# A graph attention layer: exponentials straight from kept h, a third bank for h, and a new order of every engine's opening

## The chip, the cores and the metric

One core of a Trainium2 chip runs the whole layer. The metric is the device time of the execution in microseconds, taken several times; a profiled execution gives the trace.

## What is computed

The input x has 4096 rows (nodes) of 256 features, adj is a 4096 x 4096 0/1 matrix with about 1 in 256 set.

```
hn  = max(layernorm(x), 0)
h   = hn @ W.T                     # 4096 x 256
src = h @ a1;  dst = h @ a2
e   = leaky_relu(src[:, None] + dst[None, :], 0.2)
e   = where(adj == 0, -9e15, e)
out = x + softmax(e, axis=1) @ h
```

The kernel uses exp(leaky_relu(s + d)) = max(exp(s + d), exp(0.2 (s + d))). With a common factor taken out, the weight of an edge is p_scale(d) * max(c(s), g(d)), where c = exp(-0.8 s - bias), g = exp(0.8 d + bias) and p_scale = exp(0.2 d + bias') up to the constants; bias comes from an upper bound of all d, so that nothing overflows. The row's sum of weights is an extra column of the product.

## The kernel before

The 4096 nodes are 32 tiles of 128 (T = 32). The first stage (the opening) makes h; the second (the products) makes attention @ h in NG = 4 groups of RB = 8 row blocks, each group running over all 32 tiles.

**The opening, for each tile t.** VectorE takes mean and variance (`stats_of`, `gather`). For a batch of tiles (`BATCHES`: 0-1, 2-3, 4-7, 8-11, 12-17, 18-23, 24-31) ScalarE takes the root (`std_of`), VectorE its reciprocal (`rstd_of`) and, for batches that ScalarE normalises from, `shift_of`. `normalise` writes hn_sb; the lists `BY_VECTOR`, `BY_SCALAR` and `BY_GPSIMD` say on which engine. TensorE transposes the tile into a PSUM bank (`turn`). ScalarE writes the fp16 high part with Relu (`split_hn_hi`), VectorE the low part (`split_hn_lo`). TensorE projects with three products, high part by the weights' high part (`project_hi`), high by low (`project_w_lo`), low by high (`project_lo`), two matmuls each, into a bank for h: 6 or 7 in turn, so that `project_hi(t)` waits until `keep_h(t - 2)` has emptied it. ScalarE's `keep_h` writes h_sb, whose columns F and F + 1 are s and d. `value_hi` and `value_lo` make the fp16 parts of h in pairs of tiles, the operands of the products; `HIGH_BY_SCALAR` and `HIGH_BY_GPSIMD` say who does the first.

**The weights W.** TensorE transposes W at the start. ScalarE scales it into w_hi in two halves and two extra columns (L531, L534, L537), VectorE makes w_lo of each. The instruction for w_lo's extra columns waits for `w_hi_ready` to reach KC = 2, that is for both halves.

**The turn to the products.** When h of tile 27 is kept, VectorE takes the largest d so far (d_up, L935), TensorE spreads it and the d of the last four tiles (`turn_d`, `spread_d`), and VectorE makes d_top, d_early, d_safe and exp_bias. `exp_c` turns s of the first 8 row blocks, which came back by way of DRAM into c_row, into c, in four parts. Two VectorE instructions make the arguments for g and p_scale of tiles 0 to 3 in gp_args, and one Exp on ScalarE (`exp_gp`) makes both; the same again for tiles 4 to 31 later. A small Exp on table_ready (L620) stands ahead of keep_h(28).

**The products.** For each tile VectorE makes p_sb = min(max(c, g), adjacency bits) (`weights_part`, `edge_weights`), ScalarE p_hi = p_sb * p_scale (`hi_part`, `split_hi`), VectorE p_lo (`low_part`, `split_lo`), and TensorE adds 8 x 3 products of 257 or 256 columns (`sums`). Tiles 0 and 1 are done in parts, to start sooner. adj is loaded by SyncE into a ring of four slots, each as soon as the weights of the tile four earlier are made. For the later groups c is computed once for all tiles (c_col), transposed by VectorE (c_blocks), stored by GpSimd to c_flat and loaded by SyncE into c_row between the adjacency loads.

Every engine runs its own program, written out instruction by instruction up to the end of group 0, and waits on semaphores. ScalarE, VectorE, GpSimd and TensorE take their instructions strictly in the written order. The later groups run in loops that the change does not touch.

## Time and profile before

| | |
|---|---|
| median of 3 runs | 384.48 us (384.39 to 384.5) |
| profiled execution | 384.67 us, span 382.9 us |
| TensorE busy | 376.8 us (98%) |
| VectorE busy | 363.9 us (95%) |
| ScalarE busy | 195.1 us (51%) |
| GpSimd busy | 42.0 us (11%) |
| first product starts | 40.84 us |

The span is the stretch from the first to the last instruction of the trace, and the execution's time holds some 1.8 us more. In rows of a timeline the first number is the start in us from the span's start, the second the time from there to the end of the group, then engine, line, operation, output<-inputs, the shape and how many instructions are merged; brackets give the idle time before and what ended it. PE is TensorE, PEld its weight loads, ACT ScalarE, DVE VectorE, POOL GpSimd, SP SyncE.

### The profile page before, as it was taken

The numbers are of one execution on the slowest core, as the hardware profiler recorded it, in microseconds if no ns is written. First come the engines' busy times: TensorE is split into PE (matmuls) and PEld (weight loads), VectorE is DVE, ScalarE is ACT, GpSimd is POOL, SyncE is SP. The second block draws the span as 40 slices with busy tenths as digits, with TensorE's granted clock in tenths as the row PEclk, the third lists the DMA queues.
The fourth block names the chain that finished last, engine by engine and source line by source line (L and its number), as shares of the span: only waits on it lengthen the run. The fifth ranks groups of instructions, "written<-read, shape, count | busy, mean of one in ns | idle before, by whom it ended". The sixth has DMA issues, their size and how long they took to land.

```text
span 382.9 us, 9216 instructions
## 1 busy us (share of the span) xinstructions
PE 376.8 (98%) x3358; PEld 330.7 (86%) x3358; DVE 363.9 (95%) x458; ACT 195.1 (51%) x271; POOL 42.0 (11%) x66
## 2 busy tenths in 40 slices
PE   8999899999999999999999999999999999999996
PEld 6788688888888888888888888888888888888885
DVE  4999999999999999999999999999987999999965
ACT  5899754744443644344445544444446443444330
POOL 3897020000000001110000002100000012100000
PEclk9999999999999999999999999999999999999999
DMA  7922476847676666776676667766665577766503
GB/s 241 370 78 56 130 235 218 287 154 238 217 236 208 205 220 214 243 229 218 220 223 207 209 217 233 236 222 225 215 205 184 168 222 240 232 220 221 165 2 110
DMA packets 27024, 78.22 MB, mean 204 GB/s; under 512 B 3956, under 2 KB 9336, under 8 KB 27000
## 3 DMA queue, kind: packets, MB, share of 16 engines
q1 hardware_dynamic: 25712, 74.72, 60.9%
q0 software_dynamic: 1280, 3.16, 2.2%
q8 instruction: 16, 0.26, 0.3%
q14 instruction: 8, 0.07, 0.1%
q10 hardware_dynamic: 8, 0.00, 0.0%
HBM read 73.66 MB, written 4.21 MB: 203 GB/s over the span
## 4 chain that ended last, share of the span: by engine, by line
PE 96%; ACT 1%; DVE 1%; DMA 1%; issue 1%; ACTq 0%
PE ps L1390 87%; PE ps L1214 2%; PE ps L1229 2%; PE ps L1235 2%; PE ps L1240 2%; DMA a_rows<-a 1%; PE ps L1179 1%; PE ps L1195 1%; DVE rows_sb L1119 0%; ACT c_row L494 0%; ACT h_sb L468 0%; ACT L620 0%; ACT p_hi L504 0%; ACTq L479 0%; DVE inv_den L1115 0%
## 5 line engine op out<-in xcount | busy, mean ns | idle before, releaser
L1390 PE MATMUL ps<-v_sb,p_hi 128*128 (+2 forms) x2048 | 251.8, 273 | 1.0 <-ACT p_hi L504 0.9
L514 ACT ACTIVATE p_hi<-p_sb,gp 128x1024 f16<-128x1024 f32 x126 | 144.4, 1149 | 166.6 <-DVE p_sb L785 140.0
L1390 PEld LDWEIGHTS ps<-v_sb,p_hi 128*128 128x128 f16 x2048 | 199.6, 98 | 26.9 <-issue 1.2
L792 DVE SCALAR_TENSOR_TENSOR p_lo<-p_sb,gp,p_hi 128x1024 f16<-128x1024 f32 x126 | 160.8, 1277 | 7.1 <-ACT p_hi L514 6.7
L785 DVE SCALAR_TENSOR_TENSOR p_sb<-c_row,gp,adj_sb 128x1024 f32<-128x1024 uint32 (+1 forms) x126 | 160.5, 1278 | 0.0
L1390 PE MATMUL ps<-v_sb,p_lo 128*128 (+1 forms) x1024 | 142.7, 273 | 0.0
L1390 PEld LDWEIGHTS ps<-v_sb,p_lo 128*128 128x128 f16 x1024 | 100.0, 98 | 12.7 <-DVE p_lo L792 0.2
L452 POOL DMA_DIRECT2D out<-rows_sb x24 | 13.0, 541 | 263.1 <-DVE rows_sb L1086 262.9
L401 POOL TENSOR_SCALAR hn_sb<-x_sb,moments,rstd 128x256 f32<-128x256 f32 x17 | 21.3, 1261 | 4.3 <-DVE rstd L734 3.4
L744 DVE SCALAR_TENSOR_TENSOR hnt_lo<-ps,hnt_hi 128x256 f16<-128x256 f32 x32 | 12.9, 410 | 0.5 <-ACT hnt_hi L484 0.5
L1229 PE MATMUL ps<-w_hi,hnt_hi 128*128 128x258 f16 x64 | 12.5, 277 | 0.5 <-ACT h_sb L468 0.4
L468 ACT ACTIVATE h_sb<-ps 128x258 f32<-128x258 f32 x32 | 12.3, 388 | 1.1 <-PE ps L1240 1.1
L1235 PE MATMUL ps<-w_lo,hnt_hi 128*128 128x258 f16 x64 | 12.5, 277 | 0.0
L484 ACT ACTIVATE hnt_hi<-ps 128x256 f16<-128x256 f32 x32 | 12.1, 391 | 0.7 <-PE ps L1214 0.5
L725 DVE BATCH_NORM_STATS2 stats<-x_sb 128x6 f32<-128x256 f32 x32 | 12.3, 409 | 0.2 <-DMA x_sb<-x 0.2
L1240 PE MATMUL ps<-w_hi,hnt_lo 128*128 128x258 f16 x64 | 12.3, 274 | 0.0
L1214 PE MATMUL ps<-ident_a,hn_sb 128*128 128x128 f32 x64 | 12.0, 285 | 0.0
L1086 DVE SCALAR_TENSOR_TENSOR rows_sb<-rows_sb,inv_den,x_sb 128x256 f32<-128x256 f32 x24 | 11.4, 477 | 0.0
L757 DVE TENSOR_TENSOR v_sb<-h_sb,v_sb 128x512 f16<-128x512 f32 x16 | 10.8, 680 | 0.0
L686 ACT ACTIVATE rows_sb<-ps 128x257 f32<-128x257 f32 x24 | 7.9, 388 | 2.5 <-PE ps L1390 2.5
L1214 PEld LDWEIGHTS ps<-ident_a,hn_sb 128*128 128x128 f32 x64 | 7.8, 145 | 1.3 <-ACT hn_sb L475 0.6
L475 ACT ACTIVATE hn_sb<-x_sb,shift,rstd 128x256 f32<-128x256 f32 x14 | 8.5, 607 | 0.1
(85 smaller groups left out, 87.3 us busy)
## 6 DMA issues: line engine op xcount, KB each, us to landing
adj_sb<-adj_t SPq DMA_DIRECT2D x128, 512.0 KB, 4.8
x_sb<-x SPq DMA_DIRECT2D x7, 512.0 KB, 8.3
out<-rows_sb POOLq DMA_DIRECT2D x24, 128.0 KB, 4.3
c_row<-c_flat SPq DMA_DIRECT2D x3, 512.0 KB, 6.1
out<-rows_sb SPq DMA_DIRECT2D x8, 128.0 KB, 1.7
x_sb<-x SPq DMA_DIRECT2D x2, 256.0 KB, 3.8
c_row<-s_flat SPq DMA_DIRECT2D x1, 512.0 KB, 3.8
w_nat<-w SPq DMA_DIRECT2D x1, 256.0 KB, 2.8
```

The source lines that it names most:

```text
L401: nc.gpsimd.tensor_scalar(hn_sb[:, t % RN, :], x_sb[:, t, :], moments[:, t, 0:1], rstd[:, t:t + 1], ALU.subtract, ALU.mult).then_inc(hn_gp ...
L452: pool.dma_start(out_v[:, bass.ds(g * RB + k, 1), :], rows_sb[:, k:k + 1, 0:F])\
L468: nc.scalar.activation(h_sb[:, t, :], ps[:, bank_h + t % 2, 0:FW], ACT.Copy, scale=H_DOWN)\
L514: nc.scalar.activation(p_hi[:, u % R, :], p_sb[:, u % R, :], ACT.Copy, scale=p_scale[:, bass.ds(t, 1)])\
L744: nc.vector.scalar_tensor_tensor(out=turned("lo", t), in0=in_chunks(banks_t[t % TB]), scalar=0.0, in1=turned("hi", t), op0=ALU.max, op1=AL ...
L785: nc.vector.scalar_tensor_tensor(out=p_sb[:, u % R, :], in0=c_row[:, bass.ds(g * WG, WG)], scalar=g_col[:, bass.ds(t, 1)], in1=adj_sb[:, u ...
L792: nc.vector.scalar_tensor_tensor(out=p_lo[:, u % R, :], in0=p_sb[:, u % R, :], scalar=p_scale[:, bass.ds(t, 1)], in1=p_hi[:, u % R, :], op ...
L1214: last = nc.tensor.transpose(ps[:, banks_t[t % TB], c * P:(c + 1) * P], hn_sb[:, t % RN, c * P:(c + 1) * P], ident[:])
L1229: nc.tensor.matmul(bank_of(t), turned("hi", t)[:, c, :], w_hi[:, c, 0:FW], start=(c == 0), stop=False)
L1235: nc.tensor.matmul(bank_of(t), turned("hi", t)[:, c, :], w_lo[:, c, 0:FW], start=False, stop=False)
L1240: last = nc.tensor.matmul(bank_of(t), turned("lo", t)[:, c, :], w_hi[:, c, 0:FW], start=False, stop=(c == KC - 1))
L1390: return nc.tensor.matmul(ps[:, k, 0:width], part[:, u % R, k * P:(k + 1) * P], v_sb[:, bass.ds(t, 1), v, 0:width], start=start, stop=stop ...
```

## The change

- The two exponentials are taken by ScalarE from h_sb's column d, with scale and bias given as operands (`exp_g`, `exp_p`). gp_args and its four VectorE instructions go; one small VectorE instruction makes p_bias.
- h gets a third PSUM bank (6, 7, 4), and bank_d and bank_e become 5 and 2.
- The lists of who normalises and who makes value_hi are new, and so is the order of all instructions of ScalarE, VectorE, GpSimd and TensorE from the start to the end of group 0. GpSimd's exp_scale, den_scale and den_low now follow all its normalises and value_hi. table_ready moves into the middle of group 0.

The diff, cut to its core:

```diff
-    BY_VECTOR = [26]
-    BY_SCALAR = [0, 1] + list(range(4, 14, 2)) + [15, 19, 21, 23, 24, 25, 29]
-    BY_GPSIMD = [2] + list(range(3, 15, 2)) + [14, 16, 17, 18, 20, 22, 27, 28, 30, 31]
+    BY_VECTOR = []
+    BY_SCALAR = [1, 4, 6, 9, 10, 13, 14, 16, 19, 20, 22, 24, 26, 29, 30]
+    BY_GPSIMD = [0, 2, 3, 5, 7, 8, 11, 12, 15, 17, 18, 21, 23, 25, 27, 28, 31]
     HIGH_BY_VECTOR = []
-    HIGH_BY_SCALAR = [2, 6] + list(range(14, T, 2))
-    HIGH_BY_GPSIMD = [0, 4, 8, 10, 12]
+    HIGH_BY_SCALAR = [18, 20, 22, 24, 26, 28, 30]
+    HIGH_BY_GPSIMD = [0, 2, 4, 6, 8, 10, 12, 14, 16]
...
-        bank_w, bank_n, bank_d, bank_e = 4, 1, 4, 5
-        bank_h = 6
+        bank_w, bank_n, bank_d, bank_e = 4, 1, 5, 2
+        banks_h = (6, 7, 4)
+        HB = len(banks_h)
         banks_t = (2, 3, 1, 0)
         TB = len(banks_t)
...
+            normalise(0)
             pool.wait_ge(norms_ready, 1)
             nc.gpsimd.tensor_scalar(wa_norm[:], norms[:, 0:1], norms[:, 1:2], W_UP ** 2, ALU.mult, ALU.mult)\
                 .then_inc(pool_step, 1)
+            normalise(2)
+            normalise(3)
+            normalise(5)
+            normalise(7)
+            pool.wait_ge(wa_hi_ready, 1)
+            nc.gpsimd.tensor_copy(w2_hi[:], w_hi[:, :, F + 1:FW].to_broadcast([P, KC, P])).then_inc(w2_ready, 1)
+            value_hi(0)
+            normalise(8)
+            value_hi(2)
+            normalise(11)
+            value_hi(4)
+            normalise(12)
+            normalise(15)
+            normalise(17)
+            value_hi(6)
+            normalise(18)
+            normalise(21)
+            value_hi(8)
+            value_hi(10)
+            normalise(23)
+            normalise(25)
+            normalise(27)
+            normalise(28)
+            normalise(31)
+            value_hi(12)
+            value_hi(14)
+            value_hi(16)
             pool.wait_ge(pool_step, 1)
-            for n, factor in enumerate((-0.8, 0.8, -0.8 * H_DOWN)):
+            for n, factor in enumerate((-0.8, 0.8, -0.8 * H_DOWN, 0.2)):
                 nc.gpsimd.tensor_scalar(exp_scale[:, n:n + 1], wa_norm[:], factor / H_UP, None, ALU.mult)\
                     .then_inc(scales_ready, 1)
             pool.wait_ge(w_scale_ready, 1)
...
-            def exp_gp(tiles, n):
-                act.wait_ge(gp_args_ready, n)
-                nc.scalar.activation(gp[:, :, tiles], gp_args[:, :, tiles], ACT.Exp).then_inc(gp_ready, 1)
+            def exp_g(t0, t1):
+                act.wait_ge(c_bias_ready, 1)
+                act.wait_ge(h_kept, t1)
+                nc.scalar.activation(g_col[:, t0:t1], h_sb[:, t0:t1, F + 1], ACT.Exp,
+                                     bias=exp_bias[:, 0:1], scale=exp_scale[:, 1:2]).then_inc(g_ready, 1)
+
+            def exp_p(t0, t1):
+                act.wait_ge(p_bias_ready, 1)
+                act.wait_ge(h_kept, t1)
+                nc.scalar.activation(p_scale[:, t0:t1], h_sb[:, t0:t1, F + 1], ACT.Exp,
+                                     bias=p_bias[:, 0:1], scale=exp_scale[:, 3:4]).then_inc(p_scale_ready, 1)
...
             std_of(0)
-            act.wait_ge(w_turned, 1)
-            act.wait_ge(w_scale_ready, 1)
-            nc.scalar.activation(in_halves(w_hi)[:, 0], w_in_psum[:, 0], ACT.Copy, scale=w_scale[:, 0:1]).then_inc(w_hi_ready, 1)
-            act.wait_ge(w_turned, 2)
-            act.wait_ge(w_scale_ready, 1)
-            nc.scalar.activation(in_halves(w_hi)[:, 1], w_in_psum[:, 1], ACT.Copy, scale=w_scale[:, 0:1]).then_inc(w_hi_ready, 1)
+            split_w_hi(0)
             act.wait_ge(w_turned, KC)
             act.wait_ge(wa_scale_ready, 1)
             nc.scalar.activation(w_hi[:, :, F:FW], wa_in_psum, ACT.Copy, scale=wa_scale[:, 0:1]).then_inc(wa_hi_ready, 1)
-            normalise(0)
             std_of(1)
+            split_hn_hi(0)
             normalise(1)
-            split_hn_hi(0)
+            split_w_hi(1)
             split_hn_hi(1)
-            keep_h(0)
             std_of(2)
             split_hn_hi(2)
-            keep_h(1)
+            normalise(4)
             split_hn_hi(3)
-            normalise(4)
-            keep_h(2)
+            keep_h(0)
             normalise(6)
             split_hn_hi(4)
+            keep_h(1)
+            split_hn_hi(5)
             std_of(3)
+            keep_h(2)
...
             split_hn_hi(30)
             split_hn_hi(31)
+            keep_h(25)
+            keep_h(26)
             keep_h(27)
-            nc.scalar.activation(table_ready[:], eps_sb[:], ACT.Exp)
             keep_h(28)
             exp_c(0)
+            exp_g(0, R)
+            exp_c(1)
+            exp_p(0, R)
             keep_h(29)
-            exp_gp(slice(0, R), 1)
-            exp_c(1)
             exp_c(2)
+            exp_c(3)
             hi_part(0, 0)
-            exp_c(3)
             hi_part(0, 1)
             keep_h(30)
             hi_part(0, 2)
+            hi_part(0, 3)
             keep_h(31)
-            hi_part(0, 3)
             hi_part(1, 0)
             hi_part(1, 1)
             split_hi(2, 2, 0)
+            value_hi(18)
+            exp_g(R, T)
+            split_hi(3, 3, 0)
+            exp_p(R, T)
+            act.wait_ge(p_scale_ready, 2)
...
             act.wait_ge(c_bias_ready, 1)
             all_kept(act)
             nc.scalar.activation(c_col[:], h_sb[:, :, F], ACT.Exp, bias=exp_bias[:, 0:1], scale=exp_scale[:, 0:1])\
                 .then_inc(c_col_ready, 1)
-            exp_gp(slice(R, T), 2)
...
+            value_hi(30)
+            nc.scalar.activation(table_ready[:], eps_sb[:], ACT.Exp)
             split_hi(2, 26, 24)
...
+            def split_w_lo(c):
+                dve.wait_ge(wa_hi_ready, 1)
+                dve.wait_ge(w_hi_ready, c + 1)
+                nc.vector.scalar_tensor_tensor(out=in_halves(w_lo)[:, c], in0=w_in_psum[:, c], scalar=w_scale[:, 0:1],
+                                               in1=in_halves(w_hi)[:, c], op0=ALU.mult, op1=ALU.subtract)\
+                    .then_inc(w_lo_ready, 1)
+
...
-            dve.wait_ge(wa_hi_ready, 1)
-            for c in range(KC):
-                dve.wait_ge(w_hi_ready, c + 1)
-                nc.vector.scalar_tensor_tensor(out=in_halves(w_lo)[:, c], in0=w_in_psum[:, c], scalar=w_scale[:, 0:1],
-                                               in1=in_halves(w_hi)[:, c], op0=ALU.mult, op1=ALU.subtract)\
-                    .then_inc(w_lo_ready, 1)
-            rstd_of(1)
-            stats_of(4)
-            stats_of(5)
             dve.wait_ge(wa_scale_ready, 1)
             dve.wait_ge(w_hi_ready, KC)
             dve.wait_ge(wa_hi_ready, 1)
             nc.vector.scalar_tensor_tensor(out=w_lo[:, :, F:FW], in0=wa_in_psum, scalar=wa_scale[:, 0:1],
                                            in1=w_hi[:, :, F:FW], op0=ALU.mult, op1=ALU.subtract).then_inc(w_lo_ready, 1)
-            split_hn_lo(0)
+            split_w_lo(0)
+            rstd_of(1)
+            stats_of(4)
+            stats_of(5)
             stats_of(6)
+            stats_of(7)
             gather(4)
-            stats_of(7)
             gather(5)
             gather(6)
             gather(7)
-            split_hn_lo(1)
+            split_w_lo(1)
             stats_of(8)
             rstd_of(2)
+            split_hn_lo(0)
+            shift_of(2)
+            gather(8)
+            split_hn_lo(1)
+            stats_of(9)
             split_hn_lo(2)
-            gather(8)
-            shift_of(2)
-            stats_of(9)
             split_hn_lo(3)
             stats_of(10)
             stats_of(11)
...
+            value_lo(10)
+            value_lo(12)
             dve.wait_ge(h_kept, SOON - 1)
             nc.vector.tensor_reduce(d_most[:], h_sb[:, 0:SOON - 1, F + 1], AX.X, ALU.max).then_inc(d_most_ready, 1)
-            split_hn_lo(30)
-            split_hn_lo(31)
+            split_hn_lo(29)
             dve.wait_ge(h_kept, SOON)
...
-            dve.wait_ge(scales_ready, 5)
+            dve.wait_ge(scales_ready, 6)
             dve.wait_ge(d_safe_ready, 1)
             nc.vector.tensor_scalar(exp_bias[:], d_safe[:], exp_scale[:, 2:3], None, ALU.mult).then_inc(c_bias_ready, 1)
             dve.wait_ge(c_bias_ready, 1)
-            nc.vector.tensor_scalar(gp_args[:, 0, 0:R], h_sb[:, 0:R, F + 1], exp_scale[:, 1:2],
-                                    exp_bias[:, 0:1], ALU.mult, ALU.add).then_inc(g_args_ready, 1)
-            dve.wait_ge(g_args_ready, 1)
-            nc.vector.tensor_scalar(gp_args[:, 1, 0:R], gp_args[:, 0, 0:R], 0.25, math.log(P_UP), ALU.mult, ALU.add)\
-                .then_inc(gp_args_ready, 1)
-            value_lo(10)
+            nc.vector.tensor_scalar(p_bias[:], exp_bias[:], 0.25, math.log(P_UP), ALU.mult, ALU.add).then_inc(p_bias_ready, 1)
+            split_hn_lo(30)
+            split_hn_lo(31)
             weights_part(0, 0)
+            weights_part(1, 0)
             weights_part(0, 1)
-            weights_part(1, 0)
             weights_part(0, 2)
             weights_part(0, 3)
+            weights_part(1, 1)
             low_part(0, 0)
-            weights_part(1, 1)
             low_part(0, 1)
+            edge_weights(2, 2, 16, 0)
             low_part(1, 0)
...
+            dve.wait_ge(c_col_ready, 1)
+            nc.vector.transpose(c_blocks[:], c_col[:]).then_inc(c_blocks_ready, 1)
+            split_lo(2, 10, 8)
...
             def project_hi(t):
                 pe.wait_ge(hnt_hi_ready, t + 1)
-                if t >= 2:
-                    pe.wait_ge(*kept(t - 2))
+                if t >= HB:
...
+                pe.wait_ge(hnt_lo_ready, LAST_IN_BANK_E + 1)
                 nc.tensor.transpose(ps[:, bank_e, 0:P], d_up[:, 0:1].to_broadcast([P, P]), ident[:]).then_inc(d_turned, 1)
 
-            keep_busy(bank_h, 3)
+            keep_busy(banks_h[0], 3)
             turn(0)
             turn(1)
+            turn(2)
             project_hi(0)
+            project_hi(1)
             project_w_lo(0)
+            project_w_lo(1)
+            project_hi(2)
+            turn(3)
             project_lo(0)
-            project_hi(1)
-            project_w_lo(1)
-            turn(2)
+            project_w_lo(2)
             project_lo(1)
-            turn(3)
-            project_hi(2)
-            project_w_lo(2)
+            turn(4)
+            turn(5)
             project_lo(2)
             project_hi(3)
             project_w_lo(3)
+            turn(6)
             project_lo(3)
-            turn(4)
-            turn(5)
-            turn(6)
+            turn(7)
             project_hi(4)
             project_w_lo(4)
             project_lo(4)
-            turn(7)
             project_hi(5)
             project_w_lo(5)
...
             project_w_lo(27)
             project_lo(27)
             spread_d()
             project_hi(28)
+            turn_d()
             project_w_lo(28)
-            turn_d()
+            project_hi(29)
             project_lo(28)
-            project_hi(29)
+            project_hi(30)
+            project_hi(31)
             project_w_lo(29)
             project_lo(29)
-            project_hi(30)
             project_w_lo(30)
+            project_w_lo(31)
             project_lo(30)
-            project_hi(31)
-            project_w_lo(31)
             project_lo(31)
```

## Rows read from the trace of the kernel before

**Rows 1.** Page: busy us, share, instructions of each engine; clock in 40 slices.

```profile
PE 376.8 (98%) x3358; PEld 330.7 (86%) x3358; DVE 363.9 (95%) x458; ACT 195.1 (51%) x271; POOL 42.0 (11%) x66
...
PEclk9999999999999999999999999999999999999999
```

**Rows 2.** Timeline of TensorE, first product and two later tiles.

```profile
40.84 0.60 PE L1390 MATMUL ps<-v_sb,p_hi 128*128 128x257 f16 x4 [0.66 <-ACT p_hi L504]
...
52.55 1.92 PE L1390 MATMUL ps<-v_sb,p_hi 128*128 128x257 f16 x16
...
55.19 1.92 PE L1390 MATMUL ps<-v_sb,p_hi 128*128 128x257 f16 x16
```

**Rows 3.** Timeline of TensorE, start and end of the projections.

```profile
8.27 0.29 PEld L1214 LDWEIGHTS ps<-ident_a,hn_sb 128*128 128x128 f32 x2 [0.22 <-ACT hn_sb L475]
...
9.44 0.62 PE L1229 MATMUL ps<-w_hi,hnt_hi 128*128 128x258 f16 x2
...
9.85 0.63 PE L1235 MATMUL ps<-w_lo,hnt_hi 128*128 128x258 f16 x2
...
36.10 0.59 PE L1249 MATMUL ps<-hnt_hi,w_hi 128*128 128x512 f16 x2
```

**Rows 4.** Timeline of ScalarE at the start.

```profile
7.10 0.47 ACT L534 ACTIVATE w_hi<-ps,w_scale 128x256 f16<-128x256 f32 x1 [0.39 <-PE ps L1195]
...
8.29 0.59 ACT L475 ACTIVATE hn_sb<-x_sb,shift,rstd 128x256 f32<-128x256 f32 x1
...
9.00 0.38 ACT L484 ACTIVATE hnt_hi<-ps 128x256 f16<-128x256 f32 x1
```

**Rows 5.** Timeline of VectorE, start and end of the opening.

```profile
7.05 0.30 DVE L729 BATCH_NORM_AGGREGATE moments<-stats 128x2 f32<-128x6 f32 x2
...
7.76 0.88 DVE L818 SCALAR_TENSOR_TENSOR w_lo<-ps,w_scale,w_hi 128x256 f16<-128x256 f32 x2 [0.41 <-ACT w_hi L537]
...
8.55 0.16 DVE L734 RECIPROCAL rstd<-std 128x2 f32<-128x2 f32 x1
...
32.61 0.75 DVE L744 SCALAR_TENSOR_TENSOR hnt_lo<-ps,hnt_hi 128x256 f16<-128x256 f32 x2
...
33.27 0.68 DVE L757 TENSOR_TENSOR v_sb<-h_sb,v_sb 128x512 f16<-128x512 f32 x1
...
33.87 0.82 DVE L744 SCALAR_TENSOR_TENSOR hnt_lo<-ps,hnt_hi 128x256 f16<-128x256 f32 x2
...
36.66 0.21 DVE L935 TENSOR_SCALAR d_up<-h_sb,d_most 128x1 f32<-128x1 f32 x1 [0.24 <-ACT h_sb L468]
```

**Rows 6.** Timeline of GpSimd, its first and its last normalises.

```profile
8.81 2.47 POOL L401 TENSOR_SCALAR hn_sb<-x_sb,moments,rstd 128x256 f32<-128x256 f32 x2 [1.35 <-DVE rstd L734]
...
29.54 5.50 POOL L401 TENSOR_SCALAR hn_sb<-x_sb,moments,rstd 128x256 f32<-128x256 f32 x4 [1.08 <-DVE rstd L734]
```

**Rows 7.** Timeline of ScalarE at the turn to the products.

```profile
36.24 0.39 ACT L468 ACTIVATE h_sb<-ps 128x258 f32<-128x258 f32 x1 [0.28 <-PE ps L1240]
...
36.64 1.28 ACT L620 ACT_TABLE_LOAD   x1
...
38.34 0.60 ACT L494 ACTIVATE c_row<-c_row,exp_bias,exp_scale 128x256 f32<-128x256 f32 x1
...
46.92 0.43 ACT L639 ACTIVATE c_col<-h_sb,exp_bias,exp_scale 128x32 f32<-128x32 f32 x1
```

**Rows 8.** Timeline of VectorE at the turn to the products.

```profile
38.09 0.21 DVE L946 TENSOR_SCALAR exp_bias<-d_safe,exp_scale 128x1 f32<-128x1 f32 x1
...
39.41 2.36 DVE L766 SCALAR_TENSOR_TENSOR p_sb<-c_row,gp,adj_sb 128x256 f32<-128x256 f32 x5
...
52.48 0.20 DVE L981 STREAM_TRANSPOSE c_blocks<-c_col 128x32 f32<-128x32 f32 x1
```

**Rows 9.** Waits up to 50 us: who for whom, us in total, times, longest.

```profile
DVE hnt_lo L744 <- ACT hnt_hi L484: 0.5, 2, 0.3
...
DVE rstd L734 <- ACT std L463: 0.4, 2, 0.2
```

318 lines of the change are left out of this document (138 added, 180 removed).

## The prediction, made before the change was run

> **What bounds the kernel now.** I read the engines' shares first: TensorE is busy 98% of the span, VectorE 95% [rows 1]. Then TensorE's own timeline. In the product stage one tile of 24 products takes 2.64 us (tiles starting at 52.55 and 55.19), and this pace holds to the end of the stage, as the share of busy time says [rows 1, 2]. So nothing that happens beside the products after about 50 us is worth anything, and everything that moves their start moves the end by as much. What counts is the opening: the time at which TensorE reaches tile 4 of the products, 52.55.
>
> Backwards from there, the timelines show two places. First the turn from projection to products: ScalarE loads its table for Exp in 1.28 us at 36.64, while VectorE works out the bound on d (d_up 36.66 to exp_bias 38.09); exp_c(0) starts at 38.34, at once behind exp_bias, and the first product at 40.84 [rows 2, 7, 8]. Second the start: the first projection at 9.44 waits for transposes of tiles 0 and 1 [rows 3]. Between 9.44 and spread_d at 36.10 TensorE issues 30 transposed tiles and 28 x 3 projections, 114 pairs of matmuls. At 0.22 us a pair (a twelfth of 2.64) they need 25.1 of these 26.7 us, so 1.6 us are gaps. VectorE has still less room: over the whole opening its waits inside the tile loop are 0.5 us on hnt_hi and 0.4 us on std [rows 9].
>
> **The start, edit by edit.**
> - *normalise(0) goes to GpSimd.* It waits only for rstd_of(0) and takes 1.24 us (half of 2.47 for two, [rows 6]), so it is done by 7.7. turn(0) still comes behind keep_busy; its weight load at 8.27 had idled 0.22 for hn_sb [rows 3], so it comes at 8.05 to 8.27. Gain: at most 0.2.
> - *ScalarE takes split_hn_hi(0) and normalise(1) ahead of split_w_hi(1).* The second half of w_hi is now made at 7.10 [rows 4]. After the change it stands behind split_hn_hi(0), which starts 0.73 us behind turn(0) (8.27 to 9.00, [rows 3, 4]), so at 8.8 to 9.0, and behind normalise(1), 0.59 us [rows 4]. It starts at about 9.6 and is done near 10.1.
> - *What waits for it.* VectorE's next instruction after gather(3) (7.05, [rows 5]) is w_lo for the two extra columns, and this one waits for w_hi_ready to reach KC, that is for both halves. Behind it are queued split_w_lo(0), rstd_of(1) and all else of VectorE. So VectorE stands idle from 7.35 to about 10.1. The block of w_lo work started at 7.76 before (0.8 us ahead of rstd_of(1) at 8.55, [rows 5]); it is 2.35 late.
> - *Who waits for VectorE.* rstd_of(1) comes near 10.7, and GpSimd's normalise(2) can only then start: 10.8 to 12.05 against 8.81 to 10.05 [rows 6]. TensorE's new order has turn(2) ahead of project_hi(0), so the first projection moves from 9.44 to about 12.3. From turn(2) at 12.1 the same 114 pairs end at 37.2 at the earliest, 1.1 us later than 36.10, even if every gap vanishes.
> - *VectorE's sum.* Up to d_up its list is the old one, less normalise(26) (a tensor_scalar; I price it like a split, 0.33) and split_hn_lo(30) and (31) (two in 0.66), plus value_lo(10) and (12) at 0.60 each [rows 5]: +0.2 us. The late start is +2.35, and at best all 0.9 us of waits go [rows 9]: +1.65 to +2.55. VectorE was free for d_up at 36.42 (0.24 idle before 36.66, [rows 5]). With the lower end, as there is a long backlog to work from, d_up starts at 38.1 to 38.2: **+1.5 us**. Bounds: 1.1 (TensorE alone) and 2.5.
> - *GpSimd* gets exp_scale behind all normalises. Its last four took 5.50 us from 29.54, right behind rstd_of(6) [rows 6]. From a start near 30.4, with three value_hi (0.6) and six small ones, it ends near 39.3; exp_bias is due at 39.6. Cost nothing, with 0.3 us of cover.
>
> **The turn to the products.**
> - *table_ready leaves its place ahead of keep_h(28).* The trace has the table load directly in front of the first Exp in program order, behind the Copy of keep_h(27) [rows 7]. The first Exp is now exp_c(0), behind keep_h(28). keep_h(28) needs project_lo(28), which stands behind turn_d, which needs d_up: turn_d 38.5, then w_lo(28), hi(29), lo(28) at 39.0, keep_h(28) 0.42 later (as lo(27) to 36.24) and 0.39 long: 39.8. exp_bias is done at 38.30 + 1.5 = 39.8 too. So wherever the load stands against exp_c's own waits, it starts at 39.8 and nothing covers it; what covered it was VectorE's 1.6 us chain. exp_c(0) starts at 39.8 + 1.28 = 41.1 instead of 38.34: **+2.75 us**, of which 1.25 are the load. Bounds: 0 (load hidden after all) and 1.3.
>
> The Trainium skill ("ScalarE: Activation LUTs", what a table load costs) says a switch costs the load and a drain of about 1.4 us, some 2.7 us in all. The trace shows no such drain: keep_h(27) ends at 36.63, the load starts at 36.64, and the next activation follows the load. By the page the sum would be 1.4 us more, near 388.7; I go by the row.
>
> - *exp_g and exp_p from h_sb.* VectorE loses the argument instructions and gets p_bias; the trace has no Exp of 4 columns with two pointer operands, but c_col with 32 took 0.43 [rows 7], so 0.3 to 0.4 each. With E the start of exp_c(0), exp_g ends at E+0.9 and the first p_sb starts at E+1.0, against E+1.07 before (39.41, [rows 8]). Gain 0.1, between -0.1 and 0.3.
> - *exp_c(2) and (3) ahead of hi_part(0,0).* The first product comes at E+3.5 instead of E+2.5, but the next parts follow without the old gaps. 96 products of four tiles take 10.5 us; old: tile 4 starts at E+14.2 [rows 2]; new: 3.5 + 10.5 + about 0.25 = E+14.25. VectorE's list up to split_lo(3) is as long in both orders, so it forbids more. Cost 0.05, between -0.3 and 0.5.
> - *Third bank for h.* It takes away TensorE's 0.4 us wait for keep_h(29) at the end, but TensorE then idles longer for p_hi. Nothing.
> - *c_col and its transpose later.* Transpose at 52.48 before [rows 8]; after, only ahead of split_lo(2, 10). GpSimd's store of c_flat follows it, and SyncE waits for that store before it loads c_row and, behind it, the adjacency tiles from 16 on. These loads may now come late and stop VectorE ahead of split_lo(14); I bound the gap that reaches TensorE by half a tile, 1.3 us [rows 2], and take 0, since a tile's VectorE work is shorter than TensorE's and a lead has built up by then.
>
> **Sum.** +2.75 + 0.05 = +2.8 us. The profiled execution took 384.67 with a span of 382.9 (1.8 us outside it); after: span 385.7, 387.5. The median of the runs is 0.19 below the profiled one: 387.3.
>
> **Rivals.**
> - *One of the two costs is not paid.* If the load is hidden: +1.55, 386.0. If VectorE's late start is made good elsewhere and only the load shows: +1.3, 385.8. Against the first: the row order of load and Exp; against the second: only 0.9 us of waits are there to win back. 17%.
> - *TensorE's clock.* At the start it runs at the lower level (1.2 GHz): the pairs of 258 columns at 9.44 and 9.85 start 0.41 us apart against 0.22 in the product stage [rows 2, 3], though the page's clock row shows 9 in every slice [rows 1]. It rose behind these first projections. After the change it pauses from about 8.6 to 9.7 and 10.2 to 12.1, and again for some 3 us ahead of the first product. If the first 17 pairs after 12.1 run at the lower level, TensorE's chain gets 3.2 us longer; 1.1 us of this is covered by VectorE's being later: +2 us, 389.3, and with a low level at the first products up to 390.5. For it: the pauses are longer than any in the opening before. Against it: even the old 0.7 us pause ahead of the first product [rows 2] cost nothing, and the pauses are short against the work around them. 20%. This is also what the Trainium skill's clock-gate page ("TensorE: Matmul & The Clock Gate", the HAM clock gate) would have: an idle array falls to half rate and must be busy again before it is released.
> - *The layout wins.* It goes faster if split_w_hi(1) is made before about 8.0, so that VectorE isn't stopped, and the load is covered: then VectorE's 0.9 us of waits and 0.1 of exp_g are won, 383.5. For it: TensorE has 1.6 us of gaps to give. Against it: the wait for KC stands in the program order. 8%. With one of them, or both costs halved, it lands within the measurement's reach, 384.5 to 385.2: 7%.
> - *Forecast:* 387.3, its own range 386.4 to 388.5: 48%.
>
> **Range and chances.** 385.2 to 389.6 takes in the forecast, all of the first rival and two thirds of the second: 8 in 10. A measurement tells 0.2% (0.8 us): faster 0.08, same 0.07, slower 0.85.
>
> **What would show it.** VectorE idle from 7.4 to about 10 ending on ACT w_hi; normalise(2) at 10.8; first projection after 12; a table load that starts at 39 to 40 behind a Copy and ends where exp_c(0) begins; d_up at 38.2; no gap in the products from tile 1 on. Wrong: w_hi's second half before 8.5; a load that lies beside the d chain; first projections after 12 at 0.41 us a pair (the second rival); a gap in the products at tile 14 to 16.

## The result, and the profile after

The changed kernel takes 392.61 us in the median of 6 runs (392.3 to 393.58), the kernel before 384.44 (384.29 to 384.56) on the same chip: a ratio of 1.0216, 95% interval 1.0203 to 1.0229. Forecast were 387.3 and a range of 385.2 to 389.6. The sign was right, the size was not: +8.2 us against +2.8.

The page of the changed kernel, engines and TensorE's granted clock, beside [rows 1]:

```profile
PE 378.0 (97%) x3358; PEld 332.6 (85%) x3358; DVE 363.9 (93%) x454; ACT 195.5 (50%) x270; POOL 45.5 (12%) x71
...
PEclk9999999999999999999999999999999999999999
```

The work of each engine is what it was; the span grew from 382.9 to 391.0. So the 8.1 us are waiting. TensorE's timeline says where (idle time before the row, and what ended it, in brackets):

```profile
9.78 0.69 PE L1220 MATMUL ps<-ident_a,hn_sb 128*128 128x128 f32 x2 [0.96 <-ACT hn_sb L481]
12.27 0.69 PE L1220 MATMUL ps<-ident_a,hn_sb 128*128 128x128 f32 x2 [1.80 <-POOL hn_sb L403]
12.76 1.07 PE L1235 MATMUL ps<-w_hi,hnt_hi 128*128 128x258 f16 x4
...
15.33 0.64 PE L1246 MATMUL ps<-w_hi,hnt_lo 128*128 128x258 f16 x2
15.76 0.64 PE L1241 MATMUL ps<-w_lo,hnt_hi 128*128 128x258 f16 x2
...
17.29 0.38 PE L1246 MATMUL ps<-w_hi,hnt_lo 128*128 128x258 f16 x2
17.51 0.38 PE L1235 MATMUL ps<-w_hi,hnt_hi 128*128 128x258 f16 x2
...
32.31 0.38 PE L1235 MATMUL ps<-w_hi,hnt_hi 128*128 128x258 f16 x2 [1.51 <-ACT h_sb L474]
...
49.30 2.04 PE L1398 MATMUL ps<-v_sb,p_hi 128*128 128x257 f16 x16 [2.92 <-ACT p_hi L516]
...
59.96 1.92 PE L1398 MATMUL ps<-v_sb,p_hi 128*128 128x257 f16 x16
...
131.70 0.38 PE L1398 MATMUL ps<-v_sb,p_hi 128*128 128x257 f16 x2 [0.33 <-DVE p_lo L814]
```

Read the steps from one start to the next. The pairs at 15.33 and 15.76 lie 0.43 us apart, those at 17.29 and 17.51 0.22: the lower level of TensorE's clock (1.2 of 2.4 GHz) lasts to about 17, though the page's clock row has a 9 in every slice. TensorE was at this level ahead of the two pauses already: turn(0) at 8.19 is a pair of 128 columns in 0.63 us, against 0.38 for such a pair from 17.95 on. In the kernel before it left the level near 10.5 ([rows 3]: pairs at 9.44 and 9.85, 0.41 us apart). Tile 4 of the products starts at 59.96 instead of 52.55 [rows 2], the last tile of group 0 at 131.70 instead of 123.65: 7.41 us are lost before tile 4 and 0.64 inside group 0.

VectorE of the changed kernel, beside [rows 5, 8]:

```profile
10.20 0.22 DVE L840 SCALAR_TENSOR_TENSOR w_lo<-ps,wa_scale,w_hi 128x4 f16<-128x4 f32 x1 [2.84 <-ACT w_hi L495]
...
10.73 0.16 DVE L749 RECIPROCAL rstd<-std 128x2 f32<-128x2 f32 x1
...
15.99 0.42 DVE L759 SCALAR_TENSOR_TENSOR hnt_lo<-ps,hnt_hi 128x256 f16<-128x256 f32 x1 [1.31 <-ACT hnt_hi L490]
...
31.93 0.42 DVE L759 SCALAR_TENSOR_TENSOR hnt_lo<-ps,hnt_hi 128x256 f16<-128x256 f32 x1 [1.37 <-ACT hnt_hi L490]
...
42.86 0.21 DVE L952 TENSOR_SCALAR d_up<-h_sb,d_most 128x1 f32<-128x1 f32 x1
...
44.54 0.21 DVE L963 TENSOR_SCALAR exp_bias<-d_safe,exp_scale 128x1 f32<-128x1 f32 x1 [0.35 <-POOL den_low L448]
```

ScalarE of the changed kernel, beside [rows 4, 7]:

```profile
9.63 0.46 ACT L495 ACTIVATE w_hi<-ps,w_scale 128x256 f16<-128x256 f32 x1
...
31.51 0.38 ACT L490 ACTIVATE hnt_hi<-ps 128x256 f16<-128x256 f32 x1 [1.64 <-PE ps L1220]
...
44.16 0.39 ACT L474 ACTIVATE h_sb<-ps 128x258 f32<-128x258 f32 x1 [1.32 <-PE ps L1246]
44.56 1.28 ACT L506 ACT_TABLE_LOAD   x1
45.85 0.60 ACT L506 ACTIVATE c_row<-c_row,exp_bias,exp_scale 128x256 f32<-128x256 f32 x1
```

From these rows and [rows 2, 5, 7] the loss has four terms: d_up 6.20 late (42.86 against 36.66), from d_up to exp_c(0) 1.31 more (2.99 against 1.68), from there to tile 4 0.10 less (14.11 against 14.21), and 0.64 in group 0.

### The profile page after: what moved, and what is told of

Its sections match the earlier page's. It is cut to its first block, busy times and chain, and to the rows that moved or that the text cites. A ratio compares the mean times of both kernels' runs of the same rounds, so it can differ in the third digit from the quotient of the medians.

```text
span 391.0 us, 9221 instructions
## 1 busy us (share of the span) xinstructions
PE 378.0 (97%) x3358; PEld 332.6 (85%) x3358; DVE 363.9 (93%) x454; ACT 195.5 (50%) x270; POOL 45.5 (12%) x71
## 4 chain that ended last, share of the span: by engine, by line
PE 73%; DVE 16%; issue 6%; ACT 2%; POOL 1%; DMA 1%; ACTq 0%; DVEq 0%; POOLq 0%
PE ps L1398 65%; DVE p_lo L814 7%; DVE p_sb L807 7%; PE ps L1220 2%; PE ps L1235 2%; PE ps L1241 2%; PE ps L1246 2%; POOL hn_sb L403 1%; DVE v_sb L779 1%; DMA a_rows<-a 1%; DVE p_lo L800 1%; PE ps L1185 1%; PE ps L1201 1%; DVE rows_sb L1125 0%; ACT h_sb L474 0%
## 5 line engine op out<-in xcount | busy, mean ns | idle before, releaser
L1220 PE MATMUL ps<-ident_a,hn_sb 128*128 128x128 f32 x64 | 12.9, 299 | 3.1 <-POOL hn_sb L403 2.2
L740 DVE BATCH_NORM_STATS2 stats<-x_sb 128x6 f32<-128x256 f32 x32 | 12.3, 407 | 0.0
L1235 PEld LDWEIGHTS ps<-w_hi,hnt_hi 128*128 128x128 f16 x64 | 6.3, 102 | 3.7 <-ACT hnt_hi L490 1.7
```

The lines of the kernel that those rows point to most:

```text
L1220: last = nc.tensor.transpose(ps[:, banks_t[t % TB], c * P:(c + 1) * P], hn_sb[:, t % RN, c * P:(c + 1) * P], ident[:])
L1235: nc.tensor.matmul(bank_of(t), turned("hi", t)[:, c, :], w_hi[:, c, 0:FW], start=(c == 0), stop=False)
```

## The experiments

Times are medians with the lowest and highest run. The kernel before stood at 384.4 to 384.5 in every comparison. Names with a_ start from the changed kernel, with b_ from the kernel before.

### The two predicted costs, and the clock

**a_whi**: the second half of w_hi directly behind the first.

```diff
             split_w_hi(0)
+            split_w_hi(1)
...
             normalise(1)
-            split_w_hi(1)
```

> The changed kernel with split_w_hi(1) back directly behind split_w_hi(0). Theory (the late half of w_hi holds VectorE from 7.4 to 10.2, and by that the first projections and the rise of TensorE's clock): VectorE's idle 2.8 us goes, the first projection comes near 9.5, the lower clock level ends near 10.5 instead of 17, d_up comes near 37 to 37.5 instead of 42.9, and the time is 386.8 to 387.5 (what stays is the bare load, 1.3, and 0.6 in group 0). Rival (the new order of the tile loop is itself slower, the start explains only VectorE's 2.4 us): 390.

Measured: 387.12 (386.21 to 387.75), ratio 1.0068 [1.0048, 1.0088]. TensorE of a_whi, and then VectorE:

```profile
9.89 0.75 PE L1235 MATMUL ps<-w_hi,hnt_hi 128*128 128x258 f16 x4
...
42.74 3.51 PE L1398 MATMUL ps<-v_sb,p_hi 128*128 128x257 f16 x16 [2.92 <-ACT p_hi L516]
```

```profile
36.30 0.21 DVE L952 TENSOR_SCALAR d_up<-h_sb,d_most 128x1 f32<-128x1 f32 x1
```

One moved instruction gives 5.5 us back, and in this profile d_up comes 0.36 earlier than in the kernel before. So the 6.2 us ahead of d_up go with this one instruction, and the rest of the new order up to there costs nothing by itself. They are not all its own, though: a_whi_busy below, the same program up to project_lo(31), has d_up at 39.37 in its profile. The first 16 products now take 3.51 us, 2.04 in the changed kernel's profile.

**a_busy**: 3 and 5 matmuls on a matrix of ones, whose result nobody reads, between the first transposes.

```diff
             turn(0)
+            keep_busy(banks_h[0], 3)
             turn(1)
+            keep_busy(banks_h[0], 5)
             turn(2)
```

> The changed kernel with three idle matmuls (keep_busy) between turn(0) and turn(1) and five between turn(1) and turn(2), so that TensorE has hardly a pause there; VectorE's late start stays. Theory (TensorE's low clock level up to 17.1 costs about as much as VectorE's two waits of 1.3 and 0.4 us): projections of 258 columns at 0.22 us a pair from about 12.8 on, and 390.5 to 391. Rival (the clock costs nothing, since VectorE is behind anyway): level rises, time stays within 0.4 of 392.6. If the level doesn't rise with it, the pauses were not its cause.

Measured: 389.68 (387.6 to 390.21), ratio 1.0117 [1.0086, 1.0148]. TensorE of a_busy, then VectorE:

```profile
12.03 0.60 PE L1235 MATMUL ps<-w_hi,hnt_hi 128*128 128x258 f16 x4
12.47 0.60 PE L1241 MATMUL ps<-w_lo,hnt_hi 128*128 128x258 f16 x4
...
14.46 0.38 PE L1246 MATMUL ps<-w_hi,hnt_lo 128*128 128x258 f16 x2
```

```profile
9.68 0.22 DVE L840 SCALAR_TENSOR_TENSOR w_lo<-ps,wa_scale,w_hi 128x4 f16<-128x4 f32 x1 [2.42 <-ACT w_hi L495]
...
39.40 0.21 DVE L952 TENSOR_SCALAR d_up<-h_sb,d_most 128x1 f32<-128x1 f32 x1
```

And its ScalarE:

```profile
28.03 0.38 ACT L490 ACTIVATE hnt_hi<-ps 128x256 f16<-128x256 f32 x1 [0.97 <-PE ps L1220]
```

VectorE's stop is there as before, but the pairs run at the upper level from 12.03 on (0.44 for two pairs), and d_up comes 3.46 us earlier. Not all of that is the clock. The first projection comes 0.73 earlier (12.03 against 12.76). From there to project_lo(2), at 14.46 here and at 17.29 in the changed kernel, another 2.10 are won, and this is the clock. The last 0.63 come behind it, and ScalarE's stop ahead of split_hn_hi(18) is 0.67 shorter (0.97 against 1.64; the section on this stop is below). So 2.74 remain with the clock up, a stop of 0.97 among them. The time gave more than I had expected, 2.9 instead of 1.6 to 2.1 us.

**b_whi**: the same late half in the kernel before, and nothing else of the change.

```diff
-            act.wait_ge(w_turned, 2)
-            act.wait_ge(w_scale_ready, 1)
-            nc.scalar.activation(in_halves(w_hi)[:, 1], ...)
...
             normalise(1)
             split_hn_hi(0)
+            act.wait_ge(w_turned, 2)
+            act.wait_ge(w_scale_ready, 1)
+            nc.scalar.activation(in_halves(w_hi)[:, 1], ...)
             split_hn_hi(1)
```

> The kernel before with only the second half of w_hi moved from 7.1 to behind split_hn_hi(0) and normalise(1). Theory (this one move holds VectorE, GpSimd and the first projection): VectorE idle some 2.3 us up to 10, d_up 1.5 to 2.5 us later, 386 to 387. Rival (it hurts only with the new TensorE order, which puts turn(2) ahead of project_hi(0)): under 385.

Measured: 386.11 (384.88 to 388.34), ratio 1.0047 [1.0025, 1.007]. VectorE of b_whi:

```profile
9.31 0.48 DVE L818 SCALAR_TENSOR_TENSOR w_lo<-ps,w_scale,w_hi 128x256 f16<-128x256 f32 x1 [1.60 <-ACT w_hi L541]
...
39.18 0.21 DVE L935 TENSOR_SCALAR d_up<-h_sb,d_most 128x1 f32<-128x1 f32 x1 [0.24 <-ACT h_sb L468]
```

A stop of 1.60 us moves d_up by 2.52: here too d_up moves by more than the stop's length. The profile names what stands beside it: TensorE's pairs are 0.43 us apart up to 13.6 instead of 10.5, and ScalarE stands still for 0.76 us ahead of 28.18.

**a_table**: table_ready back ahead of keep_h(28). **b_table**: it is taken out of the kernel before.

```diff
             keep_h(27)
+            nc.scalar.activation(table_ready[:], eps_sb[:], ACT.Exp)
             keep_h(28)
...
             value_hi(30)
-            nc.scalar.activation(table_ready[:], eps_sb[:], ACT.Exp)
```

> The changed kernel with table_ready back ahead of keep_h(28). Theory (the load of the Exp table lies bare on the path from keep_h(28) to exp_c(0)): the load starts right behind keep_h(27), beside VectorE's d chain, exp_c(0) starts with exp_bias, and the time falls by 1.2 to 1.3 us, from 392.6 to 391.3. Rival (exp_c(0) is held by exp_bias, which waits for GpSimd's scales until 44.5): the gain is under 0.9, since exp_bias at 44.75 lets exp_c(0) start no sooner than 44.8 against 45.85.

> The kernel before without table_ready: the first Exp is exp_c(0) behind keep_h(28). Theory: the load starts behind keep_h(28), which follows project_lo(28) at 37.1, so at 37.9 instead of 36.64, and ends at 39.2 against exp_bias at 38.3: +0.9 us, 385.3. Rival (load hidden wherever it stands): 384.4.

Measured: a_table 391.41 (390.63 to 391.98), ratio 1.018 [1.0162, 1.0198]; b_table 385.34 (384.41 to 385.74), ratio 1.0015 [1.0006, 1.0025]. ScalarE of a_table, then of b_table:

```profile
42.18 1.28 ACT L635 ACT_TABLE_LOAD   x1
...
44.13 0.60 ACT L506 ACTIVATE c_row<-c_row,exp_bias,exp_scale 128x256 f32<-128x256 f32 x1 [0.17 <-DVE exp_bias L963]
```

```profile
37.11 0.39 ACT L468 ACTIVATE h_sb<-ps 128x258 f32<-128x258 f32 x1 [0.88 <-PE ps L1239]
37.52 1.28 ACT L494 ACT_TABLE_LOAD   x1
38.81 0.60 ACT L494 ACTIVATE c_row<-c_row,exp_bias,exp_scale 128x256 f32<-128x256 f32 x1
```

The load lies bare where it follows keep_h(28), and costs 1.2 us of the median in the changed kernel, 0.8 in the kernel before. In a_table exp_c(0) starts 1.93 us behind d_up (42.20 to 44.13), against 2.99 in the changed kernel and 1.68 in the kernel before: of the 1.31 on this way 1.06 are the load, and 0.25 stay, since exp_bias still waits for GpSimd's scales.

### The stop of ScalarE near 31

turn(18) was issued at 29.3 and yet split_hn_hi(18) starts at 31.51, behind 1.64 us of idle time. An instruction packet of queue q14 lies in this stretch. In the trace's DMA view of single microseconds (packets, MB, share of 16 engines), the changed kernel has from 26 to 27:

```profile
q14 instruction: 1, 0.01, 19.1%
```

A share of 19.1% of 16 engines over 1 us is 3.06 us. The queue's packet of 21 to 22 took 0.32 (2.0%), and the packet at 20 to 21 of the kernel before 0.42. The long one falls into the time in which SyncE's store of s to s_flat, 1024 pieces of 4 bytes, is under way (issued at 22.96). **a_near** stores 8 rows of 512 bytes in its place; c of group 0 is then not the reference's.

```diff
-            sp.dma_start(s_flat.rearrange("t p -> p t"), h_sb[:, 0:RB, F], ...)
+            sp.dma_start(s_flat, h_sb[0:RB, 0, 0:P])
```

> The changed kernel with another store into s_flat: 8 rows of 512 bytes (the first 128 features of 8 nodes) in place of 1024 single numbers of 4 bytes, so the c values of group 0 and its output are not the reference's. Theory (ScalarE's stop of 1.6 to 1.8 us ahead of split_hn_hi(18), for which its semaphore had long been ready, is its instruction stream arriving late: the packet of the instruction queue takes 3.1 to 3.4 us instead of 0.3 when it falls among the small packets of that store): that packet takes under 0.6 us, the stop ahead of split_hn_hi(18) goes, VectorE's wait of 1.4 near 31 and TensorE's of 1.5 near 32 with it, and the time is 391.0 to 391.3. Rival (the stop comes from the order, through a semaphore): stop and time as in the changed kernel, 392.6.

Measured: 390.96 (390.87 to 391.32), ratio 1.0166 [1.0131, 1.0201]. The same stretch of a_near, and then its VectorE:

```profile
q14 instruction: 1, 0.01, 3.1%
```

```profile
32.09 0.20 DVE L749 RECIPROCAL rstd<-std 128x8 f32<-128x8 f32 x1 [0.24 <-ACT std L469]
...
40.71 0.21 DVE L952 TENSOR_SCALAR d_up<-h_sb,d_most 128x1 f32<-128x1 f32 x1
```

The packet takes 0.50 us, the stop is gone, d_up is 2.15 earlier and the time 1.65 lower. Of the 2.15, 0.43 are there at project_lo(2) already (16.86 against 17.29), so the stop is worth 1.7, about its own length of 1.64. The time shows less than it gave, since the first 16 products of this profile took 3.50 us. That the scattered store stretched the packet is shown; that ScalarE stood still because its instructions had not arrived is inferred. A long packet isn't enough either: a_all_busy below has one of 2.8 us and no such stop. Nor is the new order needed for it: b_whi, in the old order, has a packet of 3.04 us and a stop of 0.76.

### All repairs, and what remains

**a_all**: a_whi, a_table, and edge_weights(7, 31) ahead of split_lo(6, 30) on VectorE at the end of group 0, as in the kernel before (the diff shows the third move, and the line that a_all_busy adds). **a_all_busy**: a_all with 8 further matmuls whose result nobody reads, ahead of the first product. **a_whi_busy**: a_whi with 12 of them there.

```diff
             value_lo(30)
-            split_lo(6, 30, 24)
             dve.wait_ge(p_lo_ready, 28)
             edge_weights(7, 31, 128, 0)
+            split_lo(6, 30, 24)
...
             project_lo(31)
+            keep_busy(0, 8)
```

> The changed kernel with three repairs: split_w_hi(1) behind split_w_hi(0), table_ready ahead of keep_h(28), and edge_weights(7, 31) ahead of split_lo(6, 30) at the end of group 0. Theory (the three costs are separate): from a_whi's 387.1 another 1.0 for the load and 0.5 for group 0, 385.5, and up to 1.5 less if the shorter pause ahead of the first products keeps TensorE's clock up: 384.0 to 385.6. Rival (the rest of the order costs over 1 us besides): over 386.

> a_all with 8 matmuls on the identity, whose result nobody reads, between the last projection and the first product: TensorE's pause of 1.8 us there is filled. Theory (VectorE and ScalarE set the pace of group 0's tiles, as p_hi and p_lo come): the first 16 products may be faster, the fifth tile starts at the same time, 384.5 as a_all. Rival (what TensorE lost by a lower clock after the pause is carried to the end): 0.5 to 1.3 us gained, 383.2 to 384.0.

> a_whi (the changed kernel with split_w_hi(1) early) with 12 idle matmuls between project_lo(31) and the first product. Theory (in a_whi's trace the first 16 products take 3.5 us instead of 2.0, as TensorE's clock fell over the pause of 2.9 us ahead of them): with the pause filled they take 2.0, and the time is 385.7 to 386.4 against 387.1. Rival (the slow products are covered, since VectorE's p_lo sets the pace up to tile 3): within 0.3 of 387.1.

Measured: a_all 384.52 (383.66 to 387.53), ratio 1.0007 [0.9982, 1.0032]; a_all_busy 384.77 (384.26 to 388.21), 1.0035 [1.0012, 1.0057]; a_whi_busy 387.1 (386.05 to 390.18), 1.0084 [1.0051, 1.0118]. TensorE of a_all:

```profile
42.14 2.04 PE L1398 MATMUL ps<-v_sb,p_hi 128*128 128x257 f16 x16 [1.79 <-ACT p_hi L516]
...
52.79 1.92 PE L1398 MATMUL ps<-v_sb,p_hi 128*128 128x257 f16 x16
```

Three moves bring tile 4 to within 0.24 us of the kernel before, and the median to it. So the loss goes with these three places; the rest of the new layout is worth nothing that these runs can measure (a_all's interval reaches from -0.7 to +1.2 us). The matmuls ahead of the products brought nothing here. One of a_all's ten times and five of a_all_busy's eleven lie above 386, and no profile was taken of one of them.

In a_whi_busy the times fell in two groups (386.1 to 387.1 and 389.4 to 390.2). Its profile is from the upper one. TensorE and VectorE of a_whi_busy:

```profile
14.40 0.38 PE L1246 MATMUL ps<-w_hi,hnt_lo 128*128 128x258 f16 x2
```

```profile
39.37 0.21 DVE L952 TENSOR_SCALAR d_up<-h_sb,d_most 128x1 f32<-128x1 f32 x1
```

Up to project_lo(31) this is the program of a_whi, and w_hi is early in both. Yet here the pairs lie 0.43 us apart up to 13.5, project_lo(2) comes 1.94 later than in a_whi (12.46), ScalarE has a stop of 1.02 ahead of 28.02, and d_up is 3.07 later: about the sum of the two. So the lower level and the stop cost about what they last, also without the late half of w_hi, and they come in some executions of one program and not in others. The profile says nothing on the first products' price (2.04 us).

**a_best**: a_all with GpSimd's scale instructions back at the start, behind normalise(2).

> a_all (the changed kernel with w_hi's second half directly behind the first, the table load behind keep_h(27), edge_weights(7, 31) ahead of split_lo(6, 30)) with GpSimd's seven scale operations put back to the start, behind normalise(2). Theory: VectorE's wait of 0.36 us for den_low ahead of exp_bias goes, and with it 0.3 us of the way to the first product, if the seven operations (about 0.2 us each) don't make hn of tile 3 late: 384.2 against 384.5 of a_all. Rival 1: normalise(3) is pushed later by over 1 us, the first projections starve and the lower clock stays for longer: 385.5 to 387. Rival 2: the first p_hi, not exp_bias, sets the first product, and nothing moves.

Measured: 387.18 (385.78 to 387.85), ratio 1.0062 [1.0043, 1.0081]. The time is in the first rival's range; TensorE of a_best:

```profile
12.93 0.44 PE L1220 MATMUL ps<-ident_a,hn_sb 128*128 128x128 f32 x2 [1.14 <-POOL hn_sb L403]
```

Seven small instructions ahead of normalise(3) stop TensorE for 1.14 us, d_up comes at 40.0 instead of 36.75. The other half of that rival does not hold: the pairs are at the upper level from 10.97 on, and what stands beside the wait is a stop of ScalarE of 1.58 us ahead of 28.61. Late scales are the better place, and cost a wait of 0.35 us at exp_bias.

### The end of group 0, and the first products

**a_end**: the changed kernel with the move at the end of group 0 alone. **after_again**, **a_end_again**: the changed kernel and a_end once more, side by side. **a_fill**: the changed kernel with 13 matmuls ahead of the first product.

> The changed kernel, only split_lo(6, 30) moved behind edge_weights(7, 31) at the end of group 0, as the kernel before has it. Theory: the idle time of TensorE of 0.33 us ahead of the last product of group 0 at 131.7 goes and group 1 starts 0.4 to 0.5 us earlier, 392.0 to 392.3 against 392.6. Rival: the half microsecond belongs to the slower first products of group 0, and the next wait takes its place: 392.6, no change.

> The changed kernel once more, as the yardstick of this call for a_end_again and a_fill. 392.3 to 394; if the lower level at the first products comes in some executions only, single times stand in two groups some 1.3 to 1.5 us apart.

> The same kernel as a_end (edge_weights(7, 31) ahead of split_lo(6, 30)), beside the changed kernel in one call. Theory: its own worth is 0.4 to 0.5 us less than after_again, and a_end's 394.1 was the lower level at the first products. Rival: the order itself costs, 1 us or more above after_again.

> The changed kernel with 13 matmuls on a matrix of ones, whose result nobody reads, between the last projection and the first product. Theory (an idle time of 2.9 us ahead of the products lets TensorE's clock fall in some executions): the first 16 products take 2.0 us in every profile, the upper group of times loses its 1.3 to 1.5 us: 0.3 to 1.3 us below after_again. Rival (what falls at the first products is hidden, since p_hi and p_lo of the next tiles come later than TensorE needs them): within 0.2 us of after_again.

Measured: a_end 394.14 (391.81 to 394.84), 1.0238 [1.0213, 1.0262]; after_again 394.54 (393.12 to 395.69), 1.0258 [1.0238, 1.0279]; a_end_again 393.98 (392.48 to 394.57), 1.0231 [1.0211, 1.0251]; a_fill 393.29 (390.98 to 394.49), 1.0212 [1.0186, 1.0237]. TensorE of after_again, then of a_fill:

```profile
32.16 0.64 PE L1241 MATMUL ps<-w_lo,hnt_hi 128*128 128x258 f16 x2
32.59 0.64 PE L1246 MATMUL ps<-w_hi,hnt_lo 128*128 128x258 f16 x2
...
49.62 3.31 PE L1398 MATMUL ps<-v_sb,p_hi 128*128 128x257 f16 x16 [2.92 <-ACT p_hi L516]
```

```profile
50.78 2.04 PE L1399 MATMUL ps<-v_sb,p_hi 128*128 128x257 f16 x16
...
133.51 0.38 PE L1399 MATMUL ps<-v_sb,p_hi 128*128 128x257 f16 x2 [0.67 <-DVE p_lo L814]
```

The same program was 1.9 us slower here than in the first comparison, at a mean granted clock of 0.987 to 0.991 instead of 1.00, and its first 16 products took 3.31 us instead of 2.04. Behind 2.9 us of idle time TensorE thus starts the products at either level. The two profiles are 0.97 us apart (393.63 and 392.66): d_up is 0.32 later, the first 16 products take 1.27 more, and 0.64 of it come back inside group 0. What the rest of the 1.9 us between the medians is, no profile shows. d_up's 0.32 has more than one part too. The lower level at the start ended near 15 instead of 17, but ScalarE's stop was 2.17 us, and behind TensorE's idle time of 2.05 us that goes with it the pairs lie 0.43 us apart once more, up to about 35. The profiles of a_end, a_end_again and a_fill have the same second slow stretch, behind 2.06, 2.21 and 2.40 us; the changed kernel's first profile, behind 1.51, has not. From tile 4 to the last tile of group 0, 71.10 us pass in the kernel before and in both runs of a_end, and 71.10 also in after_again, where the lower level had delayed the products; 71.74 in the changed kernel, 71.73 in a_table, 72.07 in a_fill, where they began at the upper level. a_all and a_all_busy, with the move and at the upper level, take 71.36 and 71.25. So the order at the end of group 0 costs 0.4 to 0.8 us, but only where the products started at full rate: the two losses cover each other. Both profiles of a_end started at the lower level, so they could not show what the move is worth. Between the medians (after_again, a_end_again, a_fill) the differences of 0.6 and 1.2 us lie inside the spread of the runs.

### What the change names first

**b_bank_exp2**: the kernel before with exp_g, exp_p and the third bank, all orders else as they were. **b_fill**: the same with 8 matmuls ahead of the first product.

> The kernel before with the named content of the change alone: g and the scale of p by exp from kept d, the third bank for h, the banks of the extra transposes with it; every order otherwise as it was. Theory (only the orders cost): the third bank gives nothing, because no product waited for a bank of h; two operations of VectorE leave its list before the first edge weights, so the first product comes some 0.1 to 0.3 us earlier; 384.2 to 384.6 against 384.5. Rival (the content itself costs: exp_g and exp_p are two activations of 128x4 where one of 128x8 stood, and the wait for hnt_lo before the extra transposes, which now use a bank of hn, holds d's chain): exp_c(0) or the first product later by 0.5 us or more, 385 or above.

> b_bank_exp2 (the kernel before with the exponentials and the third bank) with 8 such matmuls between the last projection and the first product, which fill TensorE's idle time of 1.85 us. Theory (the third bank lets the last four projections run without waits, and so puts TensorE's idle time in one piece, in which the clock falls in some executions): 384.3 to 384.6 with the spread of the kernel before, 0.4 to 0.7 below b_bank_exp2. Rival (exp_g and exp_p as two activations cost it, or the wait of the extra transposes): 385.0 again.

Measured: 385.04 (384.36 to 386.01), ratio 1.0018 [1.0007, 1.0028]; b_fill 384.4 (383.73 to 385.53), ratio 1.0 [0.9991, 1.001]. TensorE of b_bank_exp2, then of b_fill:

```profile
38.84 0.38 PE L1241 MATMUL ps<-w_hi,hnt_lo 128*128 128x258 f16 x2
41.08 0.60 PE L1392 MATMUL ps<-v_sb,p_hi 128*128 128x257 f16 x4 [1.85 <-ACT p_hi L506]
```

```profile
38.93 1.95 PE L1180 MATMUL ps<-ones 128*128 128x128 f32 x16
40.95 0.60 PE L1393 MATMUL ps<-v_sb,p_hi 128*128 128x257 f16 x4
```

The third bank does what it says: the last projections run without a wait. TensorE is done a microsecond earlier than in the kernel before (its last projection started at 39.79) and idles in one piece, 1.85 us, where it had idled in short ones (0.66 ahead of the first product, [rows 2]). Five of the twelve times without the filling matmuls (385.4 to 386.0) have a mean clock of 0.995 or 0.996; with them no run is below 0.998, and the half microsecond is gone, though the two were measured on different chips and their intervals just overlap. Neither version beats the kernel before by anything that can be measured, nor does any other here. The exponentials and the bank were not run apart; together, with the idle time filled, they cost and bring nothing that can be measured.

## Why the prediction was wrong, step by step

- *w_hi's second half stops VectorE to about 10.1, normalise(2) 10.8, turn(2) 12.1, first projection 12.3.* Right: 10.20, 10.99, 12.27, 12.76.
- *"At best all 0.9 us of waits go ... with the lower end ... d_up starts at 38.1 to 38.2: +1.5 us".* This step failed: d_up is 6.2 late. Both its bounds, 1.1 (TensorE's 114 pairs at 0.22 us each) and 2.5 (VectorE's sum), took the rest of the opening as it was, or better, and so left out two things. One is TensorE's lower level, 2.1 us (a_busy) and at most 2.8, if all of its earlier first projection is put down to it. The other is ScalarE's stop ahead of split_hn_hi(18), 1.7 us (a_near). What is left for the late start itself is 1.7 to 2.4 us, an estimate from these differences; this is above the +1.5 and inside the bounds. VectorE's two long waits in the tile loop belong to the two omissions: the one of 1.31 at 15.99 is absent in a_busy, the one of 1.37 at 31.93 in a_near.
- *TensorE's clock as a rival of 20%, +2 us.* Its size for the clock was right; it should have stood in the sum. The pauses of 0.96 and 1.80 us ahead of 12.27 are those that the forecast computes. The pairs stayed 0.43 us apart up to 17, which is the case that the rival describes, for about 11 pairs, not 17. That its share came out near the +2 has some luck in it: the rival took off 1.1 us as covered by VectorE, but VectorE waited too. The level also differs between executions (a_whi against a_whi_busy), so a chance belongs to it, but every profile with w_hi late and the pauses unfilled has it. The Trainium skill's rule ("TensorE: Matmul & The Clock Gate", the HAM clock gate), that an idle array is at half rate and must be busy before it is released, agrees with these rows.
- *Missed:* a queue's instruction packet falls into the scattered store, and ScalarE stands still behind it (a_near: 1.7 us of d_up's 6.2, 1.65 of the time). No row of the kernel before shows it, where the packet took 0.42 us.
- *The table load bare behind keep_h(28), +1.25.* Right: 44.56 to 45.85, and 1.2 of the time back in a_table; on the way from d_up the load is 1.06 of the +1.31. exp_c(0) follows the load by 0.01 us; the drain of 1.4 us that the Trainium skill states ("ScalarE: Activation LUTs", What ACT_TABLE_LOAD costs) is not there, and going by the row was right.
- *First product at E+3.5, tile 4 at E+14.25.* Right: 3.45 and 14.11. This profile started its products at the upper level; in after_again, at the lower one, tile 4 comes at E+15.37.
- *GpSimd's scales at nothing, with 0.3 of cover.* Off: exp_bias waits 0.35 us for them. GpSimd's last three value_hi took 2.64 us, priced at 0.6 each. In the changed kernel the table load stood beside this wait; in a_table 0.25 us of it are left.
- *Third bank nothing.* Right for the gain, but its longer idle time costs 0.5 us in the median where nothing else is moved (b_bank_exp2, with the exponentials in it; gone in b_fill).
- *The end of group 0* was not priced at all, as the forecast held that nothing beside the products after about 50 us is worth anything: 0.64 us. The late c_col, taken at nothing, is right: TensorE's timeline shows no wait between tile 4 and 131.70.

The sum of what the profile shows, +6.20 + 1.31 - 0.10 + 0.64 = +8.05, against +2.75 + 0.05. Of the 5.25 us between them 4.7 are the one step to d_up.

The wait of w_lo's extra columns for both halves of w_hi guards more than its operand: part of the columns lies in the PSUM bank that ScalarE reads for the second half. VectorE without this wait wasn't tried.

## What to carry to other kernels

Where a step leaves TensorE idle for a microsecond or more, price the lower clock behind it as part of that step, with its chance, and not as a rival to it; read the distance of equal matmuls behind each gap, since the page's clock row may show nothing. Where a late start costs more than its own length, look for what came with it before calling it a delay that grows: here the lower clock and a stop of ScalarE, each with rows of its own, make up the difference. When a whole order is laid out anew, look first for the single instruction that moved behind a wait it did not have: three such moves undid 8 us.

## What the runs showed of the hardware

- TensorE, at the lower level before, kept it through idle times of 0.96 and 1.80 us: its pairs of 258 columns ran at 0.43 us each for some 4 us behind them. In after_again it fell from the upper level behind 2.05 us of idle time, with pairs 0.43 us apart for some 3 us. Behind 2.92 us the same program took 2.04 us for 16 products in one profile and 3.31 in another, variants of it up to 3.51. Why an execution falls in one group or the other stays open.
- One instruction packet took 3.06 us among 4-byte pieces of a store, and 0.50 when the store had pieces of 512 bytes; ScalarE's stop of 1.64 us went with it.
- With matmuls whose result nobody reads in 1.85 us of idle time ahead of the products, no execution had a mean clock below 0.998 any more, and the median was 0.6 us lower (b_fill against b_bank_exp2); in a_all_busy, where the median was 384.77 against 384.52, they brought nothing.
